# Feed forward: every other weight tile stored split by block 0 and loaded as hi and lo afterwards

## The chip, the cores and the metric

The kernel runs on one core of one Trainium2 chip. The metric is the device time of one execution in microseconds (us).

## The reference

Two sublayers on `x` of 2 x 2048 x 1024, all in fp32:

```python
x = x + attn(_layernorm(x), Wqkv, bqkv, Wo, bo)
x = x + ffn(_layernorm(x), gate_w, up_w, down_w, fc1_w, fc2_w, expert_w, ln_gamma, ln_beta)

def ffn(hidden_states, ...):
    logits = hidden_states @ gate_w
    routing_weights, _ = top_k(logits, 2)
    h = relu(hidden_states @ up_w) ** 2
    shared_out = h @ down_w
    x_latent = hidden_states @ fc1_w
    moe_out = (x_latent @ expert_w) * sum(routing_weights)
    routed_out = moe_out @ fc2_w
    return layernorm(shared_out + routed_out, ln_gamma, ln_beta)
```

Attention has one head of 256. The change is in the feed forward alone.

## The kernel before

**Precision.** Every fp32 product is made of three fp32r products: an operand is split into `hi` (the value rounded to fp32r) and `lo` (the rest), and `mm3` adds hi x hi, hi x lo and lo x hi. The split of an operand is one copy on ScalarE (`hi`) and one subtraction on POOL or DVE (`lo = source - hi`, in the helpers called `low`).

**The feed forward.** `upw` and `downs`, `down0`, `down1`, `e2d` hold the two weights; fc1 and the folded expert path run as extra columns of the up and extra rows of the down product. Each product is done by a recursive scheme with seven products in place of eight (`UP`, `DOWN` list their order). The tokens are taken in `NBK` = 4 blocks of 1024. A block has 70 steps of the up product (seven products p, ten tiles c each), then 70 steps of the down product. Step s of block n uses one weight tile of 128x512, numbered K = 140 n + s (up) or 140 n + 70 + s (down), and is 12 matmuls of 128x512 on TensorE: 4 slices or token tiles, 3 each. All four blocks use the same 140 tiles: the same weights are fetched and split in every block. The combined weights were made before, in the attention, and lie in `ups` and `downs` in DRAM. In block 3 the last product of the down product (`LAST` = 550, ten tiles) is done token tile by token tile, so its ten tiles are all kept, in `wlast`.

**The life of a weight tile.** SP fetches it into one of three `stageF` buffers (`stf`, `fetch`, L749), ScalarE makes `hi` in the ring of three pairs `wring` (`w_hi`, L971), POOL makes `lo` (`w_low` through `low`, L1992), and TensorE waits for that `lo` (`w_lo(K)`). The pair K % 3 is free when TensorE has ended step K - 3. SP issues the fetch of K + 6 in step K, after the `lo` of K + 3 has freed the buffer:

```python
w.wait_ge(*w_lo(WSEQ[i - 3]))
eng.dma_start(stageF[i % 3][:, :], src).then_inc(*d_sf[i % 3].up(K))
```

For the last product five `lo` parts are DVE's (`W_DVE`, L1559) and five are POOL's; ScalarE makes their `hi` in steps 31, 33, ... 49 of block 3's down product.

**What stands around it.** The order on each engine is written out by hand: in each step, an engine first does `turnover(K)`, which is the tile K + 3, and then the rest of the step. On ScalarE the rest is the `hi` of the activations `hr` for the down product (`hop_hi`, L990), of the operands `xop` for the up product (`x_hi`, L976), and relu and square. On DVE it is the evacuation of PSUM (`up_evac`, `down_evac`), the `lo` of `hr` (L1192), the sums of the activations of the scheme (`h_add`, L1550, in block 3; on POOL, L2076, in blocks 0 to 2), the layer norm of the block before (`tail`, L1632 and L1641) and the turned tokens. On SP it is the loads `xia` and `xib` of the next tokens from `x2d` (`load_x2`, L569, 16 DMAs of 128 KB in steps 0 to 3 and again in steps 20 to 23 of the down product), the output's stores (`store_out`, L812, which wait for DVE's `v_fin`) and the loads of the residual (`load_x1`, L808: `xr<-x1d`, in the last block also `xrz<-x1d`). All SP transfers share one DMA queue. ScalarE issues DMAs only in the attention (`e2d<-e2s`, L922).

Of the kernel before, what the change touches and what calls it, by code (L numbers as in the profile page):

```python
# [106 lines left out]
def layer(nc, x, xc, wqkv, bqkv, wo, bo, gate, upw, down0, down1, expt, fc2, gamma, beta, quad_c,  # L107
          x1d, x2d, qd, kd, vd, e2d, ups, downs, out):
    ctx = ExitStack()
    with ctx:  # L110
# [96 lines left out]
        wring = [pair(f"wr{i}", kb) for i, kb in enumerate((180, 184, 128))]  # L207
        wlast = [pair(f"wz{i}", kb) for i, kb in enumerate((20, 24, 28, 112, 116, 120, 124, 188, 52, 56))]
# [28 lines left out]
        TURN = {K: [K + 3] for K in range(LAST - 3)}  # L237
        for i, s in enumerate((31, 33, 35, 37, 39, 41, 43, 45, 47, 49)):
            TURN.setdefault(LAST - 60 + s, []).append(LAST + i)
        WSEQ = [0, 1, 2] + [k for K in sorted(TURN) for k in TURN[K]]  # L240
        WAT = {K: i for i, K in enumerate(WSEQ)}
        W_DVE = [K for K in WSEQ if K >= LAST and K % 2]
# [48 lines left out]
        a_w = ev("a_w", WSEQ)  # L291
# [6 lines left out]
        a_mid = ev("a_mid", [(t, hh) for t in (2, 3) for hh in range(2)])  # L298
        a_fin = ev("a_fin", [(t, hh) for t in (2, 3) for hh in range(2)])
# [4 lines left out]
        v_agg = ev("v_agg", range(8))  # L304
        v_dm = ev("v_dm", range(8))
# [9 lines left out]
        v_bob = ev("v_bob", [0])  # L315
# [11 lines left out]
        v_g = ev("v_g", [0])  # L327
# [12 lines left out]
        v_w = ev("v_w", W_DVE)  # L340
# [24 lines left out]
        g_w = ev("g_w", [K for K in WSEQ if K not in W_DVE])  # L365
# [22 lines left out]
        d_bo = dma("d_bo", [0])  # L388
        d_wo = dma("d_wo", [0])
# [8 lines left out]
        d_sf = [dma(f"d_sf{i}", WSEQ[i::3]) for i in range(3)]  # L398
        d_gate = dma("d_gate", [0])
# [164 lines left out]
        def _(eng):  # L564
# [121 lines left out]
            eng.dma_start(gst[:, 0, :, :], gate).then_inc(*d_gate.up(0))  # L686
# [4 lines left out]
            for c in range(8):  # L691
                b, kb = divmod(c, 4)
                for j in range(8):
# [6 lines left out]
                    if c == 7 and j == 4:  # L700
# [5 lines left out]
                        eng.dma_start(bob[:, :], bo.partition_broadcast(128)).then_inc(*d_bo.up(0))  # L706
# [198 lines left out]
        def _(eng):  # L905
# [52 lines left out]

            def w_hi(K):
                hi, _, src = w_parts(K)  # L960
                w.wait_ge(*d_sf[WAT[K] % 3][K])
                if K < 3:
                    w.wait_ge(*d_sh[2][31])
                elif K < LAST:
                    w.wait_ge(*pe_slot(K - 3))
                elif K < LAST + 8:
                    w.wait_ge(*p_up[NBK - 1, 69])
                    w.wait_ge(*v_hf[NBK - 1, "12", 9])
                else:
# [1614 lines left out]
```

## Time and profile before

| | |
|---|---|
| median of 3 runs | 2348.6 us (2348.12 to 2349.76) |
| the profiled execution's own time | 2344.41 us |
| its span, first to last instruction | 2342.5 us |
| mean granted clock of TensorE | 0.999 |
| TensorE busy | 2303.6 us, 98% |
| VectorE (DVE) busy | 1747.8 us, 75% |
| GpSimd (POOL) busy | 1571.4 us, 67% |
| ScalarE (ACT) busy | 903.4 us, 39% |
| DMA | 386.47 MB, mean 165 GB/s |

Busy time is the time in which an engine has an instruction in work, overlaps counted once. A line number is that of the helper that records the instruction, so tiles tell more than lines: `wr0h` is the `hi` of ring pair 0, `wr0l` its `lo`, `stf` the fetched tile, `hr` the split activations. SPq and ACTq are DMA issues. The time to landing runs from the issue to the moment the semaphore has its full count.

### The profile page before, as it was taken

To read this page: it belongs to the slowest core of one execution; us is meant where nothing else is said; L and a number is where in the kernel's file an instruction comes from. 1 tells how busy PE (TensorE), PEld (TensorE's weight loads), DVE (VectorE), ACT (ScalarE), POOL (GpSimd) and SP (SyncE) were. 2 spreads that over 40 slices of the span, in tenths; PEclk is the share of its full clock that TensorE was granted. 3 is DMA by queue.
4 is the path that set the end of the run, shared out by engine and by line. 5 is a ranking of instruction groups with operands and counts; after the bars stand their busy time and mean duration, and the time that the engine had idled before them with its cause. 6 is when DMAs were issued, how large, how long until landed. Compare 5 with 4: busy or idle time off the path is not lost.

```text
span 2342.5 us, 31302 instructions
## 1 busy us (share of the span) xinstructions
PE 2303.6 (98%) x11224; PEld 1919.9 (82%) x11224; DVE 1747.8 (75%) x2965; ACT 903.4 (39%) x1701; POOL 1571.4 (67%) x1175
## 2 busy tenths in 40 slices
PE   8999999999999999999999999999999999999998
PEld 7888888888998788878887887888788788878776
DVE  6989768888887526755788865479885468988978
ACT  5222243334333534434432443442344443244352
POOL 6656636655557775699567489847649975856772
PEclk9999999999999999999999999999999999999999
DMA  7989656788778633443345345435444433553342
GB/s 289 316 306 306 216 159 198 202 268 269 209 212 239 197 97 97 131 126 118 94 148 166 96 129 127 118 94 170 142 117 124 122 110 109 180 153 126 95 139 86
DMA packets 200137, 386.47 MB, mean 165 GB/s; under 512 B 19120, under 2 KB 78640, under 8 KB 198192
## 3 DMA queue, kind: packets, MB, share of 16 engines
q1 hardware_dynamic: 198832, 382.38, 54.1%
q8 instruction: 90, 1.47, 0.3%
q10 hardware_dynamic: 1152, 2.10, 0.2%
q14 instruction: 63, 0.52, 0.1%
HBM read 260.67 MB, written 90.18 MB: 150 GB/s over the span
## 4 chain that ended last, share of the span: by engine, by line
PE 56%; DVE 17%; POOL 11%; DMA 8%; issue 4%; SPq 2%; ACT 1%; DVEq 0%; POOLq 0%; ACTq 0%
PE ps L2217 18%; PE ps L2219 18%; PE ps L2218 18%; DVE pturn L1338 5%; DMA pland<-pturn 4%; POOL hq L2076 3%; SPq L641 2%; POOL wr1l L1992 2%; POOL wr0l L1992 2%; POOL wr2l L1992 2%; DVE x L1365 1%; DVE mx L1321 1%; POOL xr L2083 1%; DMA stf<-ups 1%; DMA stf<-downs 1%
## 5 line engine op out<-in xcount | busy, mean ns | idle before, releaser
L1992 POOL TENSOR_TENSOR wr0l<-stf,wr0h 128x512 fp32r<-128x512 f32 x184 | 261.8, 1423 | 146.0 <-ACT wr0h L971 145.9
L1992 POOL TENSOR_TENSOR wr2l<-stf,wr2h 128x512 fp32r<-128x512 f32 x183 | 260.7, 1425 | 142.8 <-ACT wr2h L971 142.6
L1992 POOL TENSOR_TENSOR wr1l<-stf,wr1h 128x512 fp32r<-128x512 f32 x183 | 262.6, 1435 | 137.3 <-ACT wr1h L971 137.3
L971 ACT CAST wr0h<-stf 128x512 fp32r<-128x512 f32 x184 | 114.5, 622 | 303.1 <-PE ps L2219 246.8
L971 ACT CAST wr2h<-stf 128x512 fp32r<-128x512 f32 x183 | 113.9, 622 | 303.7 <-PE ps L2219 238.8
L971 ACT CAST wr1h<-stf 128x512 fp32r<-128x512 f32 x183 | 113.8, 622 | 293.5 <-PE ps L2219 244.9
L1992 POOL TENSOR_TENSOR pt<-pland,pt 128x512 fp32r<-128x512 f32 x120 | 153.6, 1316 | 76.1 <-ACT pt L949 76.1
L939 ACT ACTIVATE prob<-ps,nm 128x512 f32<-128x512 f32 x128 | 86.2, 687 | 241.3 <-DVE nm L1329 241.3
L1338 DVE STREAM_TRANSPOSE pturn<-prob 128x512 f32<-128x512 f32 x128 | 131.7, 1090 | 60.0 <-DMA pland<-pturn 58.3
L1192 DVE TENSOR_TENSOR hr2l<-hq,hr2h 128x512 fp32r<-128x512 f32 x78 | 96.6, 1238 | 92.7 <-ACT hr2h L990 92.6
L1192 DVE TENSOR_TENSOR hr1l<-hq,hr1h 128x512 fp32r<-128x512 f32 x78 | 98.7, 1265 | 87.0 <-ACT hr1h L990 86.8
L1192 DVE TENSOR_TENSOR hr0l<-hq,hr0h 128x512 fp32r<-128x512 f32 x78 | 96.6, 1238 | 89.7 <-ACT hr0h L990 89.7
L2217 PE MATMUL ps<-pt,vh 128*128 128x256 f32 x512 | 145.2, 284 | 5.5 <-DVE pt L1192 4.6
L2219 PE MATMUL ps<-pt,vl 128*128 128x256 f32 x512 | 144.9, 283 | 0.0
L2218 PE MATMUL ps<-pt,vh 128*128 128x256 f32 x512 | 144.9, 283 | 0.0
L2076 POOL TENSOR_TENSOR hq<-hq,hq 128x512 f32<-128x512 f32 x90 | 141.2, 1569 | 0.0
L1992 POOL TENSOR_TENSOR xl<-xt,xh 128x512 fp32r<-128x512 f32 x54 | 72.0, 1342 | 73.4 <-ACT xh L929 73.2
L2038 POOL TENSOR_SCALAR x<-x,nm,rst 128x1024 f32<-128x1024 f32 x28 | 33.5, 1207 | 114.6 <-DVE rst L1206 114.6
L2217 PEld LDWEIGHTS ps<-pt,vh 128*128 128x128 f32 x512 | 98.2, 192 | 7.7 <-DVE x L1365 5.2
L2217 PE MATMUL ps<-xh,wh 128*128 128x512 f32 x256 | 101.3, 396 | 0.8 <-POOL wl L1992 0.7
L2217 PE MATMUL ps<-kh,q 128*128 128x512 f32 x256 | 100.3, 392 | 0.8 <-ACT prob L939 0.8
L2218 PE MATMUL ps<-kl,q 128*128 128x512 f32 x256 | 99.8, 390 | 0.0
(498 smaller groups left out, 7720.8 us busy)
## 6 DMA issues: line engine op xcount, KB each, us to landing
stf<-ups SPq DMA_DIRECT2D x160, 256.0 KB, 3.3
stf<-downs SPq DMA_DIRECT2D x160, 256.0 KB, 2.9
pland<-pturn SPq DMA_DIRECT2D x120, 256.0 KB, 4.7
stf<-in_upw_dram SPq DMA_DIRECT2D x120, 256.0 KB, 2.7
stf<-in_down_dram SPq DMA_DIRECT2D x88, 256.0 KB, 2.7
x<-in_x_dram SPq DMA_DIRECT2D x32, 512.0 KB, 6.8
x1d<-x SPq DMA_DIRECT2D x32, 512.0 KB, 5.7
xi<-in_xc_dram SPq DMA_DIRECT2D x7, 2048.0 KB, 8.8
```

Source lines behind the costliest of these rows:

```text
L641: eng.dma_start(land(g)[:, 512 * i + 32 * n * h:512 * i + 32 * n * (h + 1)], turned(g)[32 * i:32 * i + 32, :].rearrange("p (k s) -> p k s" ...
L939: eng.activation(prob[:, 512 * kb:512 * kb + 512], ps[:, kb, :], ACT.Exp, bias=nm[:, 0:1], scale=1.0 / 16, accum_out=rs[:, kb:kb + 1]).the ...
L971: eng.copy(hi, src).then_inc(*a_w.up(K))
L1192: eng.tensor_tensor(lo, src, hi.bitcast(F32), ALU.subtract).then_inc(*done)
L1321: eng.reduce_max(mx[:, kb:kb + 1], ps[:, kb, :], AX.X).then_inc(*v_mx.up((g, kb)))
L1338: eng.transpose(turned(g)[:, :].rearrange("p (k s b) -> p s k b", k=4, b=32)[:, 4 * kb:4 * kb + 4], prob[:, 512 * kb:512 * kb + 512].rearr ...
L1992: eng.tensor_tensor(lo, src, hi.bitcast(F32), ALU.subtract).then_inc(*done)
L2038: eng.tensor_scalar(x2n[C][i][:, :], x1t[i][:, :], nm2[:, i:i + 1], rst2[:, i:i + 1], ALU.add, ALU.mult).then_inc(*g_x2.up(g))
L2076: eng.tensor_tensor(hq[o][:, c, :], hq[a][:, c, :], hq[b][:, c, :], op).then_inc(*g_hs.up((n, name, c)))
L2217: eng.matmul(o, ah, bh, start=first, stop=False)
L2218: eng.matmul(o, ah, bl, start=False, stop=False)
L2219: return eng.matmul(o, al, bh, start=False, stop=last)
```

## The change

Block 0 still fetches and splits all its 140 tiles. 75 of them, the even K and all of K = 120 to 129 (`KEPT`), are also stored as hi and lo side by side (4 KB for each partition, 512 KB a tile) into the new DRAM tensor `wsp`, by SP, right behind the fetch in the same `turnover`. In blocks 1 to 3 the 215 tiles that repeat a kept one (`LOADED`: 75, 75 and 65) are loaded from `wsp` into the ring pair, issued from ScalarE's queue where the copy stood, and TensorE waits for the load itself (`w_ready`). The other 195 are fetched and split as before. The ten tiles of the last product are all loaded, on SP's queue (`load_last`). So that the two parts can be moved by one DMA, `wring` and `wlast` become single tensors [128, 2, 512]. A fetch now waits for the `lo` of the last split tile before it with the same K % 3; with every other tile split that is K - 6. In block 0 and for tiles 140 to 142, a copy or load into a pair whose tile was kept also waits for its store. Several semaphores are merged (`d_gate` into `d_cst`, `d_bo` into `d_wo`, `v_agg` and `v_dm`, `v_bob` and `v_g`, `a_mid` and `a_fin`, `g_mid` and `g_fin`).

```diff
-        wring = [pair(f"wr{i}", kb) for i, kb in enumerate((180, 184, 128))]
+        wring = [sb(f"wr{i}", [128, 2, 512], kb, F32R) for i, kb in enumerate((180, 184, 128))]
...
+        def kept(K):
+            n, k = divmod(K, PER)
+            return k if k < 70 else 70 + 10 * DOWN[0].index(DOWN[n][k % 70 // 10]) + k % 10
+        KEPT = [K for K in range(PER) if K % 2 == 0 or 120 <= K < 130]
+        LOADED = [K for K in range(PER, LAST) if kept(K) in KEPT]
+        SPLIT = [K for K in range(LAST) if K not in LOADED]
...
+        def w_ready(K):
+            return g_w[K] if K in g_w else d_wr[K % 3][K] if K < LAST else d_wz[0]
...
-                if i >= 3:
-                    w.wait_ge(*w_lo(WSEQ[i - 3]))
+                if K >= 3:
+                    w.wait_ge(*g_w[max(k for k in SPLIT if k < K and k % 3 == K % 3)])
...
+            def keep(K):
+                if K in KEPT:
+                    w.wait_ge(*g_w[K])
+                    eng.dma_start(wsp[K], w_both(K)[:, :, :].rearrange("p l c -> p (l c)").bitcast(F32)
+                                  ).then_inc(*d_ws[K % 3].up(K))
+            def load_last(K):
+                w.wait_ge(*d_ws[kept(K) % 3][kept(K)])
+                if K < LAST + 8:
+                    w.wait_ge(*p_up[NBK - 1, 69])
+                    w.wait_ge(*v_hf[NBK - 1, "12", 9])
+                else:
+                    w.wait_ge(*hop_at(NBK - 1, 5, 9))
+                eng.dma_start(w_both(K)[:, :, :].rearrange("p l c -> p (l c)").bitcast(F32), wsp[kept(K)]
+                              ).then_inc(*d_wz.up(0))
...
             def turnover(K):
-                for k in TURN.get(K, ()):
-                    fetch(WAT[k] + 3)
+                fetch(K + 6)
+                keep(K + 3)
+                for k in LATE.get(K, ()):
+                    load_last(k)
...
+            def w_freed(K):
+                w.wait_ge(*pe_slot(K - 3))
+                if K - 3 in KEPT:
+                    w.wait_ge(*d_ws[K % 3][K - 3])
+            def w_load(K):
+                w_freed(K)
+                w.wait_ge(*d_ws[kept(K) % 3][kept(K)])
+                eng.dma_start(w_both(K)[:, :, :].rearrange("p l c -> p (l c)").bitcast(F32), wsp[kept(K)]
+                              ).then_inc(*d_wr[K % 3].up(K))
...
             def turnover(K):
-                for k in TURN.get(K, ()):
-                    w_hi(k)
+                if K + 3 in LOADED:
+                    w_load(K + 3)
+                elif K + 3 < LAST:
+                    w_hi(K + 3)
...
             def turnover(K):
-                for k in TURN.get(K, ()):
-                    if k in g_w:
-                        w_low(k)
+                if K + 3 in SPLIT:
+                    w_low(K + 3)
```

Two places in the order of instructions. ScalarE in the down product of block 1, before; each step has the copy of a weight tile (L971) and the one of an activation tile (L990, `hq` are the activations):

```order
L990 CAST hr2h<-hq_161 128x512
L971 CAST wr2h<-stf_219 128x512
L990 CAST hr0h<-hq_161 128x512
L971 CAST wr0h<-stf_217 128x512
L990 CAST hr1h<-hq_161 128x512
```

and now (the lines are L1007 and L1026, the load is L997):

```order
L1026 CAST hr2h<-hq_162 128x512
L1007 CAST wr_173<-stf_206 128x512
L1026 CAST hr0h<-hq_162 128x512
L997 DMA wr_171<-wsp 128x1024
L1026 CAST hr1h<-hq_162 128x512
```

The copy of every other weight tile has become a DMA issue at the same place, ahead of the same activation tile.

SP in block 0, steps 19 to 23 of the down product, before; `xia` are the next block's tokens, four DMAs a row:

```order
L749 DMA stf_217<-downs 128x512
L569 DMA xia<-x2d 32x4x256 x4
L749 DMA stf_218<-downs 128x512
L569 DMA xia<-x2d 32x4x256 x4
L749 DMA stf_219<-downs 128x512
L569 DMA xia<-x2d 32x4x256 x4
L749 DMA stf_217<-downs 128x512
L569 DMA xia<-x2d 32x4x256 x4
```

and now:

```order
L758 DMA stf_204<-downs 128x512
L579 DMA xia<-x2d 32x4x256 x4
L758 DMA stf_205<-downs 128x512
L764 DMA wsp<-wr_172 128x1024
L579 DMA xia<-x2d 32x4x256 x4
L758 DMA stf_206<-downs 128x512
L579 DMA xia<-x2d 32x4x256 x4
L758 DMA stf_204<-downs 128x512
L764 DMA wsp<-wr_171 128x1024
L579 DMA xia<-x2d 32x4x256 x4
```

Two stores of 512 KB stand in the same queue between the fetches and the loads of tokens.

## Rows read from the trace of the kernel before

**Rows 1.** Busy time by stretch: the first and the last of the four blocks.

```profile
core 0: us, PE busy (x) PEld busy (x) DVE busy (x) ACT busy (x) POOL busy (x), PEclk, DMA share, GB/s
760.60:1154.00 393.40, 391.00 (x1726) 316.59 (x1724) 215.51 (x301) 169.43 (x296) 298.42 (x217) 1.00 0.45 125
...
1939.00:2332.00 393.00, 388.36 (x1707) 312.24 (x1705) 343.60 (x441) 155.29 (x269) 250.41 (x168) 1.00 0.42 128
```

**Rows 2.** Timeline of TensorE, block 1: start, length; 27 matmuls apart.

```profile
1399.80 0.39 PE L2217 MATMUL ps<-wr0h,hr1h 128*128 128x512 f32 x1
...
1405.92 0.39 PE L2217 MATMUL ps<-wr2h,hr0h 128*128 128x512 f32 x1
```

**Rows 3.** Timeline of TensorE around the gate's matmuls, block 1, step 43.

```profile
1276.18 0.39 PE L2219 MATMUL ps<-xopAh,wr0l 128*128 128x512 f32 x1
1276.50 1.90 PE L2484 MATMUL ps<-xq,gst 128*8 128x512 f32 x16
1278.33 0.50 PE L2217 MATMUL ps<-xopAh,wr1h 128*128 128x512 f32 x1
```

**Rows 4.** TensorE's waits in blocks 1 to 3: us in total, times, longest.

```profile
PE ps L2217 <- DVE hr0l L1192: 2.6, 5, 0.7
...
PE ps L2217 <- POOL wr1l L1992: 2.1, 4, 0.9
```

**Rows 5.** Costliest groups: split of a weight tile; busy, mean ns of one.

```profile
L1992 POOL TENSOR_TENSOR wr1l<-stf,wr1h 128x512 fp32r<-128x512 f32 x183 | 262.6, 1435 | 137.3 <-ACT wr1h L971 137.3
L971 ACT CAST wr0h<-stf 128x512 fp32r<-128x512 f32 x184 | 114.5, 622 | 303.1 <-PE ps L2219 246.8
```

**Rows 6.** Timeline of DVE and TensorE, block 3, step 15 of the down product.

```profile
2175.08 1.78 DVE L1550 TENSOR_TENSOR hq<-hq,hq 128x512 f32<-128x512 f32 x1
2175.30 0.47 PE L2217 MATMUL ps<-wr1h,hr0h 128*128 128x512 f32 x1 [0.40 <-DVE hr0l L1192]
...
2178.48 0.68 DVE L1550 TENSOR_TENSOR hq<-hq,hq 128x512 f32<-128x512 f32 x1
```

**Rows 7.** DMA issues by stretch, median us to landing: 1290:1340, 1195:1270, 1414:1424, 780:800, 2100:2200.

```profile
stf<-ups SPq DMA_DIRECT2D x7, 256.0 KB, 2.9
...
stf<-ups SPq DMA_DIRECT2D x25, 256.0 KB, 3.9
xr<-x1d SPq DMA_DIRECT2D x6, 512.0 KB, 4.7
...
stf<-downs SPq DMA_DIRECT2D x3, 256.0 KB, 7.2
...
stf<-in_upw_dram SPq DMA_DIRECT2D x7, 256.0 KB, 6.5
...
xrz<-x1d SPq DMA_DIRECT2D x4, 512.0 KB, 3.9
```

**Rows 8.** Timeline near the load of `xia`: first matmul of steps 21 and 31, ScalarE between.

```profile
1406.61 0.40 PE L2217 MATMUL ps<-wr0h,hr1h 128*128 128x512 f32 x1
...
1425.95 0.62 ACT L971 CAST wr1h<-stf 128x512 fp32r<-128x512 f32 x1 [2.66 <-DMA stf<-downs]
...
1438.07 0.49 PE L2217 MATMUL ps<-wr1h,hr2h 128*128 128x512 f32 x1
```

**Rows 9.** Busy time by stretch: down product of block 3, up product of block 1.

```profile
2165.00:2260.00 95.00, 92.08 (x393) 71.98 (x392) 83.32 (x79) 41.58 (x75) 72.87 (x47) 1.00 0.38 107
1200.00:1270.00 70.00, 68.70 (x301) 55.88 (x301) 69.79 (x87) 20.24 (x34) 58.62 (x37) 1.00 0.57 180
```

**Rows 10.** ScalarE's DMAs in the attention: stretch 0:760, and one issue.

```profile
e2d<-e2s ACTq DMA_DIRECT2D x8, 256.0 KB, 2.5
...
36.26 0.33 ACTq L922 DMA_DIRECT2D e2d<-e2s  x1
```

**Rows 11.** Timeline: first matmul of a step, and ScalarE's copy released by the step before.

```profile
1360.36 0.39 PE L2217 MATMUL ps<-wr1h,hr2h 128*128 128x512 f32 x1
1360.61 0.62 ACT L971 CAST wr0h<-stf 128x512 fp32r<-128x512 f32 x1 [1.58 <-PE ps L2219]
```

More of the change, by code:

```diff
@@ L107, in layer @@
 def layer(nc, x, xc, wqkv, bqkv, wo, bo, gate, upw, down0, down1, expt, fc2, gamma, beta, quad_c,
-          x1d, x2d, qd, kd, vd, e2d, ups, downs, out):
+          x1d, x2d, qd, kd, vd, e2d, ups, downs, wsp, out):
     ctx = ExitStack()
@@ L236, in layer @@
         QUARTERS = range(4)
-        TURN = {K: [K + 3] for K in range(LAST - 3)}
+        LATE = {}
         for i, s in enumerate((31, 33, 35, 37, 39, 41, 43, 45, 47, 49)):
[L239 to L242, printed above, removed]
+            LATE.setdefault(LAST - 60 + s, []).append(LAST + i)
+        def kept(K):
[4 more added lines that the diff above has]
+        SPLIT = [K for K in range(LAST) if K not in LOADED]
         XKEYS = [(n, p, j) for n in range(NBK) for p in UP for j in range(4)]
@@ L297, in layer @@
         a_oe = ev("a_oe", [(n, t) for n in range(NBK) for t in range(4)])
-        a_mid = ev("a_mid", [(t, hh) for t in (2, 3) for hh in range(2)])
-        a_fin = ev("a_fin", [(t, hh) for t in (2, 3) for hh in range(2)])
+        a_end = ev("a_end", [(of, t, hh) for of in ("mid", "fin") for t in (2, 3) for hh in range(2)])
         v_chain = Chain(sem("v_chain"))
         v_stg = ev("v_stg", STG_DVE)
-        v_agg = ev("v_agg", range(8))
-        v_dm = ev("v_dm", range(8))
+        v_mom = ev("v_mom", [(c, of) for c in range(8) for of in ("means", "deviation")])
         v_rst = ev("v_rst", range(8))
@@ L314, in layer @@
         v_bvb = ev("v_bvb", [0], 1, 2)
-        v_bob = ev("v_bob", [0])
+        v_once = ev("v_once", ["gate", "bob"])
         v_mx = ev("v_mx", [(g, kb) for g in GS for kb in QUARTERS])
@@ L364, in layer @@
         g_x2 = ev("g_x2", GS)
-        g_w = ev("g_w", [K for K in WSEQ if K not in W_DVE])
+        g_w = ev("g_w", SPLIT)
         g_x = ev("g_x", X_POOL)
@@ L371, in layer @@
                            for t in (range(8) if n < NBK - 1 else (4, 5, 6, 7, 2, 3, 0, 1))])
-        g_mid = ev("g_mid", [(t, hh) for t in (2, 3) for hh in range(2)])
-        g_fin = ev("g_fin", [(t, hh) for t in (2, 3) for hh in range(2)])
-        d_cst = dma("d_cst", [0], 2)
+        g_end = ev("g_end", [(of, t, hh) for of in ("mid", "fin") for t in (2, 3) for hh in range(2)])
+        d_cst = dma("d_cst", [0], 3)
         d_xh = dma("d_xh", [0])
@@ L397, in layer @@
                 for u in range(2)]
-        d_sf = [dma(f"d_sf{i}", WSEQ[i::3]) for i in range(3)]
-        d_gate = dma("d_gate", [0])
+        d_sf = [dma(f"d_sf{i}", [K for K in SPLIT if K % 3 == i]) for i in range(3)]
+        d_ws = [dma(f"d_ws{i}", [K for K in KEPT if K % 3 == i]) for i in range(3)]
+        d_wr = [dma(f"d_wr{i}", [K for K in LOADED if K % 3 == i]) for i in range(3)]
+        d_wz = dma("d_wz", [0], 10)
         d_gb = dma("d_gb", [0, 1])
@@ L493, in xop_of, with w_both @@
             return xopA if p in (6, 7, 4) else xopB if n else xopC
+        def w_both(K):
+            return wlast[K - LAST] if K >= LAST else wring[K % 3]
         def w_of(K):
-            return wlast[K - LAST] if K >= LAST else wring[K % 3]
+            t = w_both(K)
+            return t[:, 0, :], t[:, 1, :]
         def hslot(n, i):
@@ L685, in _ @@
             eng.dma_start(bias[:, :], bqkv).then_inc(*d_cst.up(0))
-            eng.dma_start(gst[:, 0, :, :], gate).then_inc(*d_gate.up(0))
+            eng.dma_start(gst[:, 0, :, :], gate).then_inc(*d_cst.up(0))
             for k in STG[6:15]:
@@ L727, in _, with fetch @@
                                       vv[p][:, :, 4 * kb:4 * kb + 4, :].bitcast(F32)).then_inc(*d_vsp.up(c))
-            def fetch(i):
-                if i >= len(WSEQ):
+            def fetch(K):
+                if K not in SPLIT:
                     return
-                K = WSEQ[i]
                 n, k = divmod(K, PER)
@@ L814, in turnover @@
             def turnover(K):
-                for k in TURN.get(K, ()):
-                    fetch(WAT[k] + 3)
+                fetch(K + 6)
+                keep(K + 3)
+                for k in LATE.get(K, ()):
+                    load_last(k)
+            for K in range(3):
+                keep(K)
             for n in range(NBK):
@@ L1554, in hop_low @@
                     low(hop_parts(n, i), a_hop[n, i], v_hop.up((n, i)))
-            def w_low(K):
-                for k in TURN.get(K, ()):
-                    if k in v_w:
-                        low(w_parts(k), a_w[k], v_w.up(k))
             st3_at = {}
@@ L2471, in gate_shares @@
             def gate_shares(n, u):
-                w.wait_ge(*v_g[0])
+                w.wait_ge(*v_once["gate"])
                 if u:
@@ L2577 @@
                         ("kd", (2, 4, 128, 1024)), ("vd", (2, 2, 128, 16, 128)), ("e2d", (4, 128, 2, 512)),
-                        ("ups", (10, 128, 4, 512)), ("downs", (10, 128, 4, 512))):
+                        ("ups", (10, 128, 4, 512)), ("downs", (10, 128, 4, 512)), ("wsp", (PER, 128, 1024))):
         args.append(nc.dram_tensor(name, shape, f32, kind="Internal").ap())
```

70 lines of the change are left out of this document (29 added, 41 removed).

## The prediction

> **What bounds the kernel now.** I read the busy times by stretch first. The feed forward runs from 760.6 to 2332 us in four blocks of some 393 us, of which the rows have the first and the last; TensorE is busy for 391 and 388 of them, DVE for 216 and 344, POOL for 298 and 250 [rows 1]. The reader should see that TensorE is the bound, and that only what its matmuls don't fill can be won. The timeline of TensorE says how much that is: starts 27 matmuls apart stand 6.12 us apart, 0.2267 us each [rows 2]. One weight tile is 12 matmuls, a slot of 2.72 us; a block has 140 slots, 380.9 us. The gate's matmuls open a hole of 1278.33 - 1276.18 - 0.23 = 1.9 us [rows 3], twice in a block: 4 us. Of 393 us some 8 are then lost to waits, in each block; in blocks 1 to 3, where tiles will be loaded, 23 us. The list of waits shows under half of that, since a matmul lasts 0.39 us [rows 2] and the next one's late start is idle time only beyond its end, but it names who is late: `hr*l` of DVE and `wr*l` of POOL [rows 4].
>
> Three causes lie behind those names. **POOL:** a tile costs ScalarE 622 ns and POOL 1435 ns [rows 5], and POOL also has the sums of the down product. **Shared time of DVE and POOL:** in block 3 a DVE sum takes 1.78 us with POOL at work and 0.68 us without, and between the two TensorE waits for `hr0l` [rows 6]. **Late fetches:** `stf` lands after 2.9 us in quiet stretches, 3.9 beside the output's stores and loads, 7.2 in the stretch where `xia` is loaded [rows 7]. In that stretch ScalarE sits 2.66 us for a fetch, with the cut of `hr` behind it, and ten slots take 1438.07 - 1406.61 = 31.5 us in place of 27.2 [rows 8]: 4.3 us lost.
>
> **The change, part by part.** Profiled execution: 2344.4 us, of which 2342.5 are span; the median of the runs is 4.2 us longer, and I carry that over.
>
> *Removed.* 215 of the 410 tiles of blocks 1 to 3 and all ten of the last product lose fetch, ScalarE copy and low part: 225 x 0.62 = 140 us of ScalarE, 220 x 1.43 = 315 us of POOL, 5 operations of DVE. All of it lies beside TensorE, so none of it counts by itself; what counts is the 23 us. POOL's lateness after a burst of sums goes (about 4 us with the restarts). DVE's lateness in block 3, where it is busy for 83 of 95 us and POOL for 73 [rows 9], should nearly all go, since a low part of `hr` behind POOL's tile falls by about what the sum in rows 6 does: 5 us. The late fetches of blocks 1 and 2 near `xia`, 4.3 us each by rows 8, mostly go, 6 us: SP no longer waits for the tile three slots ahead, so it fetches some slots earlier and half as often. In the up phases DVE is busy for 69.8 of 70 us [rows 9] and SP stands behind its results; lighter, I count 2 us won back, less than half of what is left. Sum: -(4 + 5 + 6 + 2) = -17 us, between 0 and all 23.
>
> *Added on ScalarE.* 215 issues, at 0.33 us for one of `e2d` [rows 10], in place of 0.62: `hr`'s cut starts some 0.2 us sooner, which is in the sum above. The price is the slack. A loaded tile may start when the slot three before has ended; ScalarE acts 0.25 us into the next slot [rows 11], and TensorE needs the tile at the end of two slots, 5.44 us, about 0.3 earlier for the weight load. So 512 KB must land within **4.9 us** of the issue. The trace has no such load on ScalarE's queue. Nearest rows: 512 KB of `xrz` behind a fetch 3.9 us, of `xr` in crowded stretches 4.7, 256 KB stored from ScalarE 2.5 [rows 7, 10]. I take 3.9 quiet (no cost) and 4.7 with a spread of half a microsecond beside the output's traffic: of about 45 loads there, 0.1 us late on the mean, 4.5 us; of the 8 us near `xia` I keep 2 for late loads. Bounds: 0 with nothing late, and 215 x 0.3 = 65 us if all of them land at 5.2.
>
> The Trainium skill ("DMA: Bandwidth & Descriptors", Issuing engines are not separate DMA queues) says that DMAs of all issuers run on the same 16 engines and that another issuer saves only the time of issuing; by it the landing would be `xr`'s 4.7 us everywhere, still within 4.9, and the sum would differ only by more loads being near the edge. It speaks against the choice of the queue, and no row here can show it.
>
> *Added in block 0.* 75 stores of 512 KB on SP's queue, each behind a fetch: 39 MB, on top of 125 GB/s [rows 1]. In quiet slots they cost nothing: a fetch has 6 us and lands in 2.9, and ScalarE's new wait for a store ends before the slot does. Crowded stretches are three: 780 to 800 us, where fetches land after 6.5 us [rows 7], and the two loads of `xia`. Two stores or more join each, in the same queue (the order of SP above). Price by block 1's stretch, 4.3 us at 7.2: from there +2 for each of the `xia` loads, +3 for the start, where `x2d` and the operands wait too. +7 us, between 0 and 3 x 4.3 = 13. Where a store is late, ScalarE's copy waits, and behind it are `hr`'s cut, DVE's low part and TensorE.
>
> *Last product.* Its ten loads are SP's, in s 31 to 49, used from s 60: nothing late. Merged semaphores: `gate`, `bo` and the moments are waited for a little later than needed, far ahead of use; nothing.
>
> Sum: -17 + 4.5 + 7 = **-5.5 us**; 2344.4 becomes 2338.9, the median 2348.6 becomes **2343.1**.
>
> **Rivals.** (1) *Loads late in crowded stretches, slower or the same.* In up phases SP, DVE and the output's traffic are late together; a copy held by its fetch (as the 2.66 us in rows 8) delays the load queued behind it, which has only 1 us to spare. Twice the 4.5 and half of the gain: -8.5 + 9 + 7 = +7.5, about 2356. It decides from a landing of some 5.0 us in those stretches. For it: `xr` at 4.7. Against: it waits there behind a fetch in one queue. (2) *Every load late.* Landing 5.2 throughout: 65 - 10 = +55, 2404 us. Against: `xrz` at 3.9. (3) *Stores hold ScalarE in block 0* beyond the 13: +15 in place of 7, 2351: the same. (4) *The gain is all that is hidden*: DVE, not the tiles, stays late; -6 + 4.5 + 7, 2354.
>
> The Trainium skill ("SBUF — State Buffer", Who interferes with whom) says that a DVE instruction with two SBUF inputs and a GpSimd instruction reading SBUF lock each other out for a whole instruction. By this rule, the trace agrees: 0.68 against 1.78 us [rows 6]; it would give rival 4 little room, since halving POOL's tiles frees DVE.
>
> **How the numbers follow.** About 0.2% (4.7 us) can be told from no change. Forecast 0.5 (of it 0.38 beyond 0.2%, 0.12 within); rival 1 0.22 (0.07 within, 0.15 slower); rival 2 0.06; rivals 3 and 4 0.22 (0.04 faster, 0.1 within, 0.08 slower). Faster 0.42, same 0.29, slower 0.29. The range: from -17 + 0 + 2 = -15, 2334, widened by 1 to 2333, up to rival 1 with block 0 at its bound, about 2363. Rival 2 and the tails are left out. The forecast's own range is 2334 to 2348.
>
> **What would show it.** In the profile after: `wr` loads on ScalarE's queue landing under 4.9 us; POOL at about 1250 us busy, DVE's low parts shorter; blocks 1 to 3 near 388 to 389 us, block 0 at about 400. I am wrong if TensorE waits for DMA `wr<-wsp` for more than some 10 us, if block 0 grows by over 13, or if DVE's waits in block 3 stay.

## The result, and the profile after

| | before | after |
|---|---|---|
| median of the runs | 2349.2 us (2348.1 to 2349.8, 4 runs) | 2371.8 us (2366.5 to 2376.8, 4 runs) |
| profiled execution: own time, span | 2344.4, 2342.5 us | 2372.1, 2370.3 us |
| mean granted clock of TensorE | 0.999 | 0.995 |
| DMA | 386.47 MB | 484.75 MB |

The changed kernel is slower: ratio 1.0099, interval 1.0086 to 1.0112. Forecast were 2343.1 us and a range up to 2363. Of all the runs told below one, of e4, was slow, 3855.1 us at a mean granted clock of 0.56, and e4's numbers leave it out. The page of the changed kernel begins with the busy times, against 2303.6 us of PE, 1747.8 of DVE, 903.4 of ACT and 1571.4 of POOL before:

```profile
PE 2310.4 (97%) x11224; PEld 1928.2 (81%) x11224; DVE 1644.9 (69%) x2960; ACT 781.3 (33%) x1476; POOL 1235.5 (52%) x955
...
wr<-wsp ACTq DMA_DIRECT2D x215, 512.0 KB, 4.3
```

POOL lost 336 us of work, DVE 103, ScalarE 122, as meant, and TensorE waits more. The last line is from the page's DMA issues: the 215 loads land after 4.3 us at the median, where the forecast had 3.9.

Where the time went is told by the busy times by stretch, one row for each block from its first matmul to the next block's first. All four of before ([rows 1] have two of them, cut a little otherwise):

```profile
core 0: us, PE busy (x) PEld busy (x) DVE busy (x) ACT busy (x) POOL busy (x), PEclk, DMA share, GB/s
760.60:1152.20 391.60, 389.20 (x1718) 315.10 (x1717) 213.71 (x298) 168.81 (x295) 297.55 (x216) 1.00 0.45 125
1152.20:1544.50 392.30, 388.49 (x1717) 315.23 (x1716) 280.96 (x358) 156.30 (x272) 284.67 (x198) 1.00 0.44 126
1544.50:1936.60 392.10, 388.94 (x1718) 315.21 (x1717) 284.24 (x358) 156.09 (x272) 284.16 (x198) 1.00 0.44 126
1936.60:2331.90 395.30, 390.75 (x1717) 314.25 (x1715) 345.95 (x444) 155.91 (x270) 251.70 (x169) 1.00 0.42 128
```

and of the changed kernel:

```profile
761.90:1162.60 400.70, 391.48 (x1717) 315.84 (x1716) 216.75 (x298) 168.11 (x294) 294.42 (x215) 1.00 0.70 221
1162.60:1559.30 396.70, 389.42 (x1717) 316.92 (x1716) 256.07 (x358) 115.76 (x197) 172.47 (x123) 1.00 0.57 175
1559.30:1958.90 399.60, 389.58 (x1718) 316.83 (x1717) 256.12 (x358) 115.74 (x197) 172.49 (x123) 1.00 0.57 173
1958.90:2359.80 400.90, 391.24 (x1717) 316.31 (x1715) 294.43 (x439) 115.56 (x196) 142.58 (x100) 1.00 0.54 175
```

The start is 1.3 us later, the blocks are longer by 9.1, 4.4, 7.5 and 5.6 us. Block 0 pays for the stores; blocks 1 to 3, which were to gain, lose 17.5. TensorE's waits in blocks 1 to 3 of the changed kernel, the whole list (us in total, times, longest):

```profile
PE ps L2247 <- DMA wr<-wsp: 26.1, 21, 3.4
PE ps L2247 <- DVE hr0l L1230: 0.6, 1, 0.6
```

Before there were waits for `hr` of 6.5 us and for `wr` of POOL of 4.3 us in all, the largest of which stand in [rows 4]. They have gone. What stands in their place are loads from the new tensor that land late.

One of them, in block 1 where `xia` is loaded, in the timeline of ScalarE (first line: its issue of the load) and of TensorE:

```profile
1364.32 0.33 ACTq L997 DMA_DIRECT2D wr<-wsp  x1
...
1376.75 0.62 ACT L1007 CAST wr<-stf 128x512 fp32r<-128x512 f32 x1 [6.01 <-PE ps L2249]
```

```profile
1369.34 0.39 PE L2249 MATMUL ps<-wr,hr1l 128*128 128x512 f32 x1
1372.06 0.50 PE L2247 MATMUL ps<-wr,hr2h 128*128 128x512 f32 x1 [2.33 <-DMA wr<-wsp]
...
1373.15 0.63 PE L2247 MATMUL ps<-wr,hr2h 128*128 128x512 f32 x1
1373.58 0.63 PE L2248 MATMUL ps<-wr,hr2h 128*128 128x512 f32 x1
```

The load was issued at 1364.32 and let TensorE go on at 1372.06: 7.7 us. SP's timeline shows its company:

```profile
1361.15 3.98 SPq L579 DMA_DIRECT2D xia<-x2d  x8
```

SP, which now has a fetch in every other step only and no longer waits there for the low part of the tile three slots ahead, issues eight loads of `xia` in a run of 4 us, most of them ahead of the weight. The median landings between 1357 and 1380 us are:

```profile
wr<-wsp ACTq DMA_DIRECT2D x4, 512.0 KB, 6.2
xia<-x2d SPq DMA_DIRECT2D x16, 128.0 KB, 5.5
```

A late load can cost more than its wait. Before the wait the matmuls stand 0.23 us apart as in [rows 2]; from 1373.15 to 1373.58 it is 0.43. The busy times by stretch show the clock there (the column PEclk, behind the five engines):

```profile
1366.00:1369.70 3.70, 3.70 (x17) 2.76 (x15) 1.40 (x2) 1.14 (x2) 1.90 (x2) 1.00 1.11 252
1369.70:1372.00 2.30, 0.03 (x1) 0.00 (x0) 0.69 (x1) 0.62 (x1) 1.06 (x1) 1.00 1.05 309
1372.00:1374.00 2.00, 1.95 (x5) 1.51 (x6) 0.00 (x0) 0.00 (x0) 0.00 (x0) 0.62 1.14 219
1374.00:1376.00 2.00, 2.00 (x6) 1.61 (x5) 0.00 (x0) 0.00 (x0) 0.00 (x0) 0.52 1.05 330
```

After 2.3 us without a matmul the granted clock falls to its lower level, 1.2 GHz in place of 2.4, and comes back some 3.3 us later: the twelve matmuls behind the wait lose 1.6 us on top of it. The matmul starts show this four times in the feed forward of the changed kernel, behind waits of 2.3, 3.4 and 2.8 us for `wr<-wsp` and one of 2.7 us for DVE in block 0; counted in the same way it costs 1.6 us behind each of the three and 1.5 behind the fourth, some 6.2 us in all. It does not follow every such wait: behind one of 2.7 us for a load, at 1769.2, the matmuls keep their 0.23 us. In the feed forward of the kernel before it does not happen at all; its longest holes are the 1.9 us of the gate [rows 3].

### The profile page after: what moved, and what is told of

The parts are those of the page before. It is cut to its first block, busy times and chain, and to the rows that moved or that the text cites. A ratio compares the mean times of both kernels' runs of the same rounds, so it can differ in the third digit from the quotient of the medians.

```text
span 2370.3 us, 30713 instructions
## 1 busy us (share of the span) xinstructions
PE 2310.4 (97%) x11224; PEld 1928.2 (81%) x11224; DVE 1644.9 (69%) x2960; ACT 781.3 (33%) x1476; POOL 1235.5 (52%) x955
## 2 busy tenths in 40 slices
DMA packets 210934, 484.75 MB, mean 205 GB/s; under 512 B 20320, under 2 KB 79840, under 8 KB 208992
## 4 chain that ended last, share of the span: by engine, by line
PE 65%; DVE 12%; DMA 12%; POOL 5%; SPq 2%; issue 2%; ACT 1%; DVEq 0%; POOLq 0%; ACTq 0%
PE ps L2247 21%; PE ps L2249 21%; PE ps L2248 21%; DMA wr<-wsp 6%; DVE pturn L1376 5%; DMA pland<-pturn 4%; POOL wr L2023 3%; SPq L651 2%; DVE x L1403 1%; DVE mx L1359 1%; DMA wsp<-wr 1%; POOL hq L2106 1%; DVE st L1410 1%; DVE st L1253 1%; PE ps L2514 1%
## 5 line engine op out<-in xcount | busy, mean ns | idle before, releaser
L2023 POOL TENSOR_TENSOR wr<-stf,wr 128x512 fp32r<-128x512 f32 x335 | 461.4, 1379 | 753.7 <-ACT wr L1007 753.5
L1007 ACT CAST wr<-stf 128x512 fp32r<-128x512 f32 x335 | 208.1, 622 | 733.1 <-PE ps L2249 648.7
L2247 PE MATMUL ps<-xopAh,wr 128*128 128x512 f32 x480 | 188.8, 393 | 3.6 <-DMA wr<-wsp 3.1
L2249 PE MATMUL ps<-xopAh,wr 128*128 128x512 f32 x480 | 187.0, 389 | 0.0
L2248 PE MATMUL ps<-xopAl,wr 128*128 128x512 f32 x480 | 186.9, 389 | 0.0
L1230 DVE TENSOR_TENSOR hr1l<-hq,hr1h 128x512 fp32r<-128x512 f32 x78 | 91.4, 1172 | 108.4 <-ACT hr1h L1026 108.3
L2247 PE MATMUL ps<-wr,hr0h 128*128 128x512 f32 x360 | 142.2, 395 | 9.2 <-DMA wr<-wsp 6.5
L2247 PE MATMUL ps<-wr,hr2h 128*128 128x512 f32 x360 | 142.2, 395 | 8.9 <-DMA wr<-wsp 7.1
L2247 PE MATMUL ps<-wr,hr1h 128*128 128x512 f32 x360 | 142.0, 394 | 8.8 <-DMA wr<-wsp 7.8
L2249 PE MATMUL ps<-wr,hr2l 128*128 128x512 f32 x360 | 141.5, 393 | 0.0
L2248 PE MATMUL ps<-wr,hr2h 128*128 128x512 f32 x360 | 141.3, 393 | 0.0
L2248 PE MATMUL ps<-wr,hr1h 128*128 128x512 f32 x360 | 140.8, 391 | 0.0
L2249 PE MATMUL ps<-wr,hr1l 128*128 128x512 f32 x360 | 140.7, 391 | 0.0
L2248 PE MATMUL ps<-wr,hr0h 128*128 128x512 f32 x360 | 140.7, 391 | 0.0
```

The source lines that it names most:

```text
L1007: eng.copy(hi, src).then_inc(*a_w.up(K))
L1230: eng.tensor_tensor(lo, src, hi.bitcast(F32), ALU.subtract).then_inc(*done)
L2023: eng.tensor_tensor(lo, src, hi.bitcast(F32), ALU.subtract).then_inc(*done)
L2247: eng.matmul(o, ah, bh, start=first, stop=False)
L2248: eng.matmul(o, ah, bl, start=False, stop=False)
L2249: return eng.matmul(o, al, bh, start=False, stop=last)
```

## The experiments

Times are medians with lowest and highest; ratios are to the kernel before, measured beside each on the same chip. Its medians there were 2348.8 us (e1 to e4), 2346.5 (e5 to e8), 2347.0 (e9 to e11) and 2347.3 (e12). The line numbers move a little with each edit.

### Which part costs: the stores, the last product, the loads (e1, e2)

```diff
-        LOADED = [K for K in range(PER, LAST) if kept(K) in KEPT]
+        LOADED = []
```

> Block 0 stores its 75 tiles, but blocks 1 to 3 fetch and split all their tiles as before; only the last product is loaded. Theory L (most of the 23 us are loads on ScalarE's queue that land after 5.1 us in crowded stretches): the stores alone cost block 0 some 9 us (400 us in place of 391) and blocks 1 to 3 are as before but for the last product; about 2349 + 9 - 2 = 2356 us. Rival S (the stores and their aftermath are most of it): 2365 us or more.

e1 took 2353.4 us (2350.2 to 2356.1), ratio 1.0017 [1.0007, 1.0028]. e2 has that edit and keeps only what the last product needs:

```diff
-        KEPT = [K for K in range(PER) if K % 2 == 0 or 120 <= K < 130]
+        KEPT = [K for K in range(120, 130)]
```

> Only ten tiles are stored (K 120 to 129) and loaded, for the last product. Theory L: block 0 is as before to 1 us, and block 3 wins 1 to 3 us of its waits for hr, since DVE loses five operations and ScalarE and POOL ten and five; 2346 to 2349 us. Rival: the ten loads of 512 KB on SP's queue delay the fetches around them, block 3 grows by 2 to 4 us, 2351 us or more.

e2 took 2346.4 us (2342.8 to 2349.7), ratio 0.999 [0.9981, 1.0]. Block 0 of e1, block 0 and block 3 of e2:

```profile
767.40:1166.00 398.60, 389.65 (x1717) 314.92 (x1716) 212.36 (x298) 168.86 (x295) 295.99 (x216) 1.00 0.71 221
```

```profile
763.70:1154.30 390.60, 388.47 (x1717) 315.27 (x1716) 212.72 (x298) 168.97 (x295) 295.97 (x216) 1.00 0.49 139
...
1936.90:2330.20 393.30, 389.59 (x1717) 314.64 (x1715) 338.66 (x439) 150.38 (x260) 243.74 (x164) 1.00 0.44 135
```

Block 0 with 75 stores is 8 us longer than with ten, and the two kernels differ by 2353.4 - 2346.4 = 7.1 us: the stores. The last product loaded in place of split gives 2.4 us, at the edge of the interval. What is left, 22.6 us of the change less 4.7 of e1, is the 215 loads of blocks 1 to 3: **18 us**, though with them the waits for POOL and DVE go.

### Less beside the load: pacing SP, leaving out the crowded steps (e3, e4)

SP was let go earlier by the change, and its fetch starts about 0.65 us before the load of the same slot. e3 holds it in step K until TensorE has ended that step:

```diff
             def turnover(K):
+                if K + 6 in SPLIT:
+                    w.wait_ge(*pe_slot(K))
                 fetch(K + 6)
```

> The change, but SP waits in each step with a fetch for TensorE's step K before it fetches K + 6, so that it can't run ahead and issue the DMAs of xia in bursts of eight. Theory B (the bursts delay the loads on ScalarE's queue): loads near xia land after 5 to 6 us in place of 7 to 9, blocks 1 to 3 win 5 to 10 us, 2362 to 2367 us. Rival V (the volume of the stretch decides, not the burst): the same as the change within 3 us, 2369 to 2375.

e3 took 2366.5 us (2362.3 to 2372.7), ratio 1.0077 [1.0053, 1.0101]. The waits fell by half, from 26.1 to 13.6 us, but the landing got worse, 4.8 us in place of 4.3: fetch and load now start in the same moment. The time came out as theory B had it, 5 us less: beside `xia` the loads took 6.0 us at the median in place of 6.9, but 13 of the 16 were still over 5.1. The list also hides a part. The matmul that ends a slot tells how much longer than 2.72 us the slot was; that excess, the gate's slots left out, I call its lateness. By it 41.5 us in blocks 1 to 3 of the changed kernel stand behind loads of over 5.1 us, and 32.6 in e3. From e3, the waits and the page's issues:

```profile
PE ps L2249 <- DMA wr<-wsp: 13.6, 18, 3.6
...
wr<-wsp ACTq DMA_DIRECT2D x215, 512.0 KB, 4.8
```

e4 splits as before in the steps around both loads of `xia` and around the loads of `x1d` in the down product; 176 loads are left:

```diff
-        LOADED = [K for K in range(PER, LAST) if kept(K) in KEPT]
+        LOADED = [K for K in range(PER, LAST) if kept(K) in KEPT and K % PER not in (*range(72, 80), *range(88, 98), *range(108, 116))]
```

> The change, but tiles of the steps around the xia loads and the x1d loads of the down product (k 72 to 79, 88 to 97, 108 to 115) are fetched and split in blocks 1 to 3 too; 52 loads fewer. Theory L: the loads' stalls there (some 22 of 32 us) go, a part comes back as late fetches; blocks 1 to 3 near 390 us each, 2355 to 2360 us in all. Rival S: within 5 us of the change, 2367 us or more.

e4 took 2357.5 us (2353.5 to 2362.2), ratio 1.0036 [1.0025, 1.0048]: 39 loads fewer bring 14 us. (The edit leaves out 39 loads and not the 52 of the expectation.) So most of the 18 us stands in those steps, but e4 is still slower than e1, and 14.8 us of waits for loads are left. By the ends of its slots 4.9 us of lateness in blocks 1 to 3 stand in steps 20 to 29 of the down products and 5.2 in steps 40 to 49, nearly all of it at two steps, 28 and 46: each is the first load behind the steps that were left out. At step 28 of blocks 1 and 2 the load took 7.5 and 7.0 us beside `xia`, which is still being loaded there; at step 46 of block 3 it took 8.3 us beside three tiles of the last product (`wz<-wsp`). So e4 moves some of the late loads rather than removing them. Waits and issues of e4:

```profile
PE ps L2247 <- DMA wr<-wsp: 14.8, 16, 3.0
...
wr<-wsp ACTq DMA_DIRECT2D x176, 512.0 KB, 4.3
```

### Spreading the loads of tokens (e5, e6, e7)

The 16 DMAs of `xia` go out four at a time in steps 0, 3, 6, 9 and 20, 24, 28, 32 in place of four steps in a row; what uses the first set moves to steps 13 to 16.

```diff
-                        if s < 4:
+                        if s in (0, 3, 6, 9):
                             w.wait_ge(*p_up[n, 69])
-                            load_x2(n + 1, 0, s)
-                        if 20 <= s < 24:
+                            load_x2(n + 1, 0, s // 3)
+                        if s in (20, 24, 28, 32):
                             w.wait_ge(*v_t2[n + 1, 0, 7])
-                            load_x2(n + 1, 1, s - 20)
+                            load_x2(n + 1, 1, s // 4 - 5)
...
-                        if 5 <= s < 9:
-                            for j in (2 * (s - 5), 2 * (s - 5) + 1):
+                        if 13 <= s < 17:
+                            for j in (2 * (s - 13), 2 * (s - 13) + 1):
```

In the kernel before:

> The kernel before, with the DMAs of xia spread out: the first half of a block's tokens in steps 0, 3, 6, 9 and its turning on DVE in 13 to 16, the second half in steps 20, 24, 28, 32. Theory C (crowding by xia makes the late fetches): fetches near xia land within 5 us, the 4.3 us of block 1, as much of block 2 and some 2 us of block 0 mostly go: 2340 to 2344 us. Rival P (POOL's burst of sums is the cause, and the late fetch only rides on it): 2347 us or more.

In the changed kernel:

> The change with the same spreading. Theory C: the loads near xia on ScalarE's queue land after 5 to 6 us in place of 6 to 9, some 12 of their 17 us of stalls in blocks 1 and 2 go: 2356 to 2361 us. Rival V (the added volume makes them late wherever they are put): 2366 us or more.

In e2:

> Only the ten tiles of the last product stored and loaded, and xia spread: the sum of the two, 2346.4 - 6 = 2338 to 2342 us, below both kernels. Rival: the two overlap, 2344 us or more.

e5 took 2343.3 us (2338.4 to 2350.8), ratio 0.9986 [0.9976, 0.9996]; e6 2362.1 (2357.1 to 2369.0), 1.0064 [1.0045, 1.0084]; e7 2337.8 (2336.6 to 2340.3), 0.9958 [0.9944, 0.9971]. Spreading is worth 3 us in the kernel before and about 8 in the changed one (from 1.0099 to 1.0064). e6 fell between its theory and its rival. In its profile, which is of its slowest run, TensorE still waits 26.7 us for `wr<-wsp`, though the longest wait is 1.9 us in place of 3.4. e7 is faster than before without any of the 215 loads of the ring; only the last product is loaded. It is also some 4 us better than e2 and e5 add up to, which no run here explains. Why spreading helps the kernel before stands in the DMA issues between 1405 and 1440 us, before (where a fetch took 7.2 us in the worst stretch of it [rows 7]):

```profile
xia<-x2d SPq DMA_DIRECT2D x16, 128.0 KB, 5.2
stf<-downs SPq DMA_DIRECT2D x6, 256.0 KB, 5.4
```

and in e5:

```profile
stf<-downs SPq DMA_DIRECT2D x6, 256.0 KB, 3.4
xia<-x2d SPq DMA_DIRECT2D x12, 128.0 KB, 3.7
```

### Which queue, and what stands beside the load (e8, e9)

e8 issues the load on SP's queue, once the slot has ended. In the order of instructions the fetch stands ahead of that wait, but it is the next fetch that goes out right behind the load, 0.36 us later. ScalarE only keeps the copies of the tiles that are split. The edit does two things: it changes the queue, and it holds all that SP issues to TensorE's steps, as e3 does.

```diff
             def turnover(K):
                 fetch(K + 6)
                 keep(K + 3)
+                if K + 3 in LOADED:
+                    w.wait_ge(*pe_slot(K))
+                    if K in KEPT:
+                        w.wait_ge(*d_ws[K % 3][K])
+                    w.wait_ge(*d_ws[kept(K + 3) % 3][kept(K + 3)])
+                    eng.dma_start(w_both(K + 3)[:, :, :].rearrange("p l c -> p (l c)").bitcast(F32), wsp[kept(K + 3)]
+                                  ).then_inc(*d_wr[K % 3].up(K + 3))
...
             def turnover(K):
-                if K + 3 in LOADED:
-                    w_load(K + 3)
-                elif K + 3 < LAST:
+                if K + 3 in SPLIT:
                     w_hi(K + 3)
```

> The change, but the 215 loads are issued by SP (which waits for TensorE's step first) in place of ScalarE. If the two queues share the engines' time between them, a load behind the xia DMAs in one queue lands later still, over 9 us near xia, and TensorE waits more: 2378 us or more. Rival (which queue a DMA is in changes nothing): within 4 us of the change's 2371.8, or of 2366.5 if SP's wait paces it as in the paced run.

e8 took 2346.0 us (2344.2 to 2355.1), ratio 1.0001 [0.9989, 1.0012], and so both halves of the expectation failed: slower than the changed kernel was forecast, and the rival had 2366 us or more. It gives back the whole loss. e9 leaves the load on ScalarE's queue and takes the fetch away from beside it: SP fetches when the last load has landed, and what stands behind the fetch waits with it.

```diff
             def turnover(K):
+                if K + 6 in SPLIT and K + 1 in LOADED:
+                    w.wait_ge(*d_wr[(K + 1) % 3][K + 1])
                 fetch(K + 6)
```

> The change with the loads still on ScalarE's queue, but SP fetches the next split tile only when the load issued last has landed. In the change the nearest fetch starts 0.65 us before the load and the load lands after 4.3 us; with SP's loads the fetch starts 0.36 us behind it and the load lands after 3.4. Theory O (the order and overlap of fetch and load decide, not the queue): the loads land after 3.4 us in the median here too, TensorE waits for wr<-wsp under 12 us, 2345 to 2352 us. Rival Q (ScalarE's queue itself is slower or treated worse): landing 4 us or more, 2360 us or more.

e9 took 2355.7 us (2353.0 to 2360.9), ratio 1.0039 [1.0027, 1.0051], between theory O and rival Q: the loads land after 3.6 us at the median, and TensorE waits 13.1 us for them. A quiet stretch, 1310 to 1350 us, shows the landing in the changed kernel

```profile
wr<-wsp ACTq DMA_DIRECT2D x8, 512.0 KB, 4.3
stf<-in_upw_dram SPq DMA_DIRECT2D x5, 256.0 KB, 3.6
```

in e8

```profile
wr<-wsp SPq DMA_DIRECT2D x8, 512.0 KB, 3.3
stf<-in_upw_dram SPq DMA_DIRECT2D x5, 256.0 KB, 3.8
```

and in e9

```profile
wr<-wsp ACTq DMA_DIRECT2D x8, 512.0 KB, 3.3
stf<-in_upw_dram SPq DMA_DIRECT2D x5, 256.0 KB, 2.6
```

So in quiet steps 512 KB of `wsp` take 3.3 us from ScalarE's queue as well, if the fetch has nearly landed when they start (it goes out 1.4 to 2 us earlier there and lands after 2.6), and SP's queue gives the same with a fetch behind the load: not the queue, the fetch that starts first takes the microsecond. In crowded steps the two differ. Between 1405 and 1440 us, in e9 (in the changed kernel 5.9)

```profile
wr<-wsp ACTq DMA_DIRECT2D x5, 512.0 KB, 5.8
xia<-x2d SPq DMA_DIRECT2D x16, 128.0 KB, 6.3
```

and in e8

```profile
wr<-wsp SPq DMA_DIRECT2D x6, 512.0 KB, 3.6
xia<-x2d SPq DMA_DIRECT2D x16, 128.0 KB, 4.3
```

A load in SP's queue stands ahead of the pieces of `xia` that SP issues later; a load in the other queue is moved beside them. It also stands behind those that SP issued before, and the median of 3.6 us hides that. Four of the six loads took 3.4 to 3.7 us; the last two, issued behind eight pieces of `xia` in a row and four more, took 8.0 and 6.6, and TensorE waited:

```profile
PE ps L2252 <- DMA wr<-wsp: 2.6, 1, 2.6
```

Over blocks 1 and 2 eight loads of e8 stand so, at 5.3 to 8.0 us, of the ten that took more than 5.1. The theory of e8's expectation was right for these eight, and wrong for the rest, which decides the time.

### Both together, and what is left (e10, e11, e12)

e10 is e8 with the tokens spread.

> Loads on SP's queue behind its wait for TensorE, and the DMAs of xia spread. Theory C: the four late loads next to xia (2 to 2.8 us each) go, as do some stalls of block 0: 2334 to 2339 us, against 2346.0 without the spreading and 2337.8 for the last product alone with it. Rival: the stores' cost in block 0 keeps it above 2341.

e10 took **2328.9 us** (2324.4 to 2332.0), ratio 0.9915 [0.9902, 0.9929]: faster than both kernels, and than the 2334 to 2339 us of its theory. Its blocks:

```profile
764.60:1160.80 396.20, 390.07 (x1717) 314.76 (x1716) 211.28 (x298) 168.08 (x294) 295.06 (x215) 1.00 0.71 223
1160.80:1546.80 386.00, 385.79 (x1717) 316.43 (x1716) 246.05 (x358) 114.37 (x197) 177.82 (x123) 1.00 0.56 179
1546.80:1932.60 385.80, 385.80 (x1718) 316.27 (x1717) 245.44 (x358) 114.35 (x197) 177.91 (x123) 1.00 0.55 179
1932.60:2319.60 387.00, 386.17 (x1717) 315.94 (x1715) 292.60 (x439) 114.12 (x196) 144.46 (x100) 1.00 0.53 181
```

Blocks 1 to 3 sum to 1158.8 us, against 1179.7 before: 20.9 us less. Four of the five or so us that are left in each over 140 x 2.72 = 380.9 us are the holes at the gate. TensorE's waits for loads in blocks 1 to 3 of e10:

```profile
PE ps L2252 <- DMA wr<-wsp: 1.0, 2, 0.8
```

e11 is e10 without the stores of steps 0 to 14 of block 0, whose start is crowded:

```diff
-        KEPT = [K for K in range(PER) if K % 2 == 0 or 120 <= K < 130]
+        KEPT = [K for K in range(16, PER) if K % 2 == 0 or 120 <= K < 130]
```

> As the run before, but the tiles K 0 to 14 are neither stored nor loaded. Block 0 starts with the crowded stretch at 780 to 800 us; without the eight stores there its up product takes 198 us in place of 201: 2331 to 2336 us, 2 to 4 below the run before. Rival (what those stores cost is regained in blocks 1 to 3 by their loads): the same within 1 us.

e11 took 2335.4 us (2330.4 to 2337.9), ratio 0.9943 [0.9931, 0.9956]: a miss. Block 0's up phase becomes 5 us shorter (202.3 to 197.1 us), but those of blocks 1 to 3 become 1.5 to 3.7 us longer each (195.6, 195.3, 196.2 to 197.5, 199.0, 197.7). Splitting these tiles again is not what costs it: over the slots 0 to 15 each of the three blocks is 2.1 us above 16 x 2.72 us in both kernels, the hole at the gate. The loss stands in the one slot behind, number 16, which takes 2.3, 3.9 and 1.5 us more than its 2.72. It uses the first load behind the run of split tiles. In e10 SP issues that load as slot 13 ends and it lands after 4.6, 5.3 and 5.1 us; in e11 the store of the output and the fetch ahead of it go out only after the slot's end, the load goes out 1.1, 1.1 and 1.9 us behind the slot's end, and it takes 6.3, 6.3 and 4.8 us. These three are nearly all of TensorE's waits for loads there:

```profile
PE ps L2252 <- DMA wr<-wsp: 5.6, 4, 2.0
```

So what a kept tile is worth against its store cannot be read from e11: it is once more a late load.

e12 is e9 with the tokens spread: ScalarE's queue, the fetch held back until the last load has landed, and a thinner crowd.

> Loads on ScalarE's queue, the split tile's fetch only after the last load has landed, and the DMAs of xia spread: the counterpart of the run with SP's loads and the same spreading (2328.9 us). If ScalarE's queue costs only because its loads share the engines with what SP has in flight (fetches and xia), little is left of the 9.7 us between the two without the spreading: 2330 to 2335 us. If the queue itself costs, the distance stays: 2338 us or more.

e12 took 2344.4 us (2334.5 to 2349.7, 12 runs), ratio 0.9984 [0.9969, 0.9999]. 15.5 us lie between it and e10. Its loads land after 3.7 us at the median over the whole run, e10's after 3.4, and the tail differs more: more than 5.1 us were taken by 41 loads in the changed kernel, 57 in e3, 45 in e6, 27 in e9, 22 in e12, 10 in e8 and 4 in e10. By the ends of the slots 15.3 us of lateness stand behind the 22 of e12 and 2.1 behind the 4 of e10, most of the distance. TensorE's waits for loads in blocks 1 to 3 of e12 are

```profile
PE ps L2249 <- DMA wr<-wsp: 8.7, 13, 1.8
```

Each of the 22 had other DMAs of SP than a fetch beside it: pieces of `xia`, stores of the output, loads of `x1d` or tiles of the last product. 124 loads of e12 had no such company, and none of them took more than 5.1 us (3.2 at the median). In e10 loads with the same company land after 3.3 to 3.8 us at the median of each kind, and in e12 after 4.0 to 4.8.

## Why the prediction was wrong

**Right: what bounds the kernel, and the gain.** The waits in the list for `hr` and for POOL's `wr` of blocks 1 to 3 fell from 10.8 to 0.6 us. POOL is busy for 1235.5 us, forecast 1250. That the gain was there to be had is shown by e10, whose blocks 1 to 3 take 20.9 us less; spreading alone gives some 3 of it by the medians of e5, or 6.4 between the profiles' blocks 1 to 3. It was even larger than the 17 us: the changed kernel's blocks 1 to 3 have 41.5 us of lateness behind late loads and are only 17.5 us longer, so that some 24 of the old waits went, all of the 23 (an estimate from these two numbers). Rival 4, that DVE stays late, is out.

**Right: the stores.** +7 us forecast, 7.1 between e1 and e2; block 0 became 9.1 us longer, under the 13 that would have told against me. Rival 3 is out.

**Right: the last product itself.** Its tiles come in time, and it is even 2.4 us better (e2), which was in the gain. What its loads do to their neighbours I had at nothing: ten loads of the ring overlap them in the changed kernel, and seven of the ten took more than 5.1 us.

**Wrong: the landing on ScalarE's queue**, the term of 4.5 us. All of the miss lies in it, and more: by the ends of the slots it measured 41.5 us in blocks 1 to 3, 35.5 of them behind the 23 loads that took more than 6 us. Three of its inputs failed:

1. *Crowded stretches*: I took 4.7 us, from `xr`, with a spread of half a microsecond. Near `xia` the loads take 5.9 and 6.2 at the median and 7.7 in the one above. The row that bore on it was there: a fetch of half the size took 7.2 us in that stretch [rows 7]. I used it as a loss that goes, and not as the price of the new load in the same place. "Of the 8 us near `xia` I keep 2" was therefore the wrong way round: a fetch of the kernel before is issued six steps ahead of its use, while the load has the end of two slots. e4, which takes 39 loads out of there and from around the loads of `x1d`, wins back 14 us.
2. *Quiet stretches*: 4.3 and not 3.9. Each load has a fetch beside it that starts 0.65 us sooner; when the fetch has nearly landed the same load takes 3.3 us (e9). `xrz` was a load behind a fetch in one queue; beside a fetch from another queue it came out slower. By itself this cost nothing, since 4.3 us is inside the budget; it left less room for what comes on top.
3. *The price of a late tile*: I counted only its lateness. Three of the waits cost another 1.6 us each at the lower clock.

The budget itself, 4.9 us, was about right: by the ends of the slots, loads that land within about 5.1 are not waited for.

This was the mechanism of rival 1, loads late in crowded stretches, but not its sizes: it gave 2356, with half of the gain kept and 9 us of lateness; the gain was kept whole, and the lateness is 41.5 us, of which TensorE's list has 26.1. Rival 2, every load late, is out: 41 of 215 were over 5.1 us, and its 2404 is far off. The sign that I named as refuting, over 10 us of waits for `wr<-wsp`, is what the trace shows.

**The choice of the queue.** e8 moves the same 215 loads, from the same place in the order of the steps, to SP's queue, and holds SP to TensorE's steps: from 1.0099 to 1.0001. Holding SP alone gives 1.0077 (e3). e9 shows that keeping the fetch out of the load's way gives 1.0039 on ScalarE's queue, and e12 against e10 that 15.5 us remain between the two queues even so, with SP held back in both, if not at the same moments. The Trainium skill ("DMA: Bandwidth & Descriptors", Issuing engines are not separate DMA queues) has DMAs of all issuers interleave on the same 16 engines. By it the trace agrees: the loads slow down with SP's transfers beside them. In these runs it also counted which queue a load was in: ahead of the `xia` pieces in SP's queue it landed after 3.4 to 3.7 us, beside them from the other queue after 5.8. That order in one queue is the reason is argued from these landings, and the late loads of e12 all having SP's company speaks for it. **Open:** whether the ordering is all of those 15.5 us, and how much of them comes from the moments at which SP is held back. No run here issues the loads from ScalarE's queue with SP's transfers held until each has landed, `xia` and the output's stores too, and none issues them on SP's queue without holding SP.

## What to carry to other kernels

Replacing work that is hidden by a transfer changes a busy engine for a deadline, so price the new transfer at the landing that the old ones have in the same place, tails first, and expect that a wait of two to three microseconds may bring the lower clock on top. Issue a transfer with a deadline first in the queue that carries its competitors, not beside them in another one, and thin out the bursts, since in that queue it also waits behind what went before. A kernel that comes out slower may still hold the gain: here 2371.8 and 2328.9 us differ only in the queue, in SP's wait for TensorE's step and in the spreading.

## What the runs showed of the hardware that I had not expected

- The landing of one and the same 512 KB load: 3.1 to 3.3 us alone, on either queue; 3.3 with 256 KB issued 0.36 us behind it in its queue; 4.3 with 256 KB started 0.65 us before it in the other; 4.4 where both start together (e3, 1310 to 1350 us); 5.8 to 6.2 at the median beside 128 KB pieces of `xia` from the other queue; 3.3 to 3.7 ahead of them in theirs, but 5.3 to 8.0 behind eight or more of them in it (e8).
- The page's mean of 205 GB/s says nothing of this. Between 1310 and 1350 us the changed kernel moves 146 GB/s on the mean, while slices of one microsecond reach 356 and others have none: the transfers run in bursts that the slots of TensorE set, and collide there.
- After four waits of 2.3 to 3.4 us in the changed kernel the granted clock fell to 1.2 GHz for some 3.3 us; after one of 2.7 us, and after the 1.9 us at the gate, it did not. The other runs widen this: it fell after one wait of 2.0 us in e11 and not after another of 2.0 in the same run, it fell after one of 1.9 us in e6, and it did not after one of 3.2 us in e9. The length of a wait alone does not tell.
